# Six of the 52 maximum units of each head move from VectorE to ScalarE copies and 16-bit folds

## The reference, cut to what matters

```python
q = split(x @ Wq + bq); k = split(ctx @ Wk + bk); v = split(ctx @ Wv + bv)
attn = softmax(q @ k.T / sqrt(8))
out = attn @ v
```

## Time and profile before

| | |
|---|---|
| median of 3 runs | 4444.05 us (4439.82 to 4445.55) |
| the profiled execution's own time | 4451.81 us |
| its span, first to last instruction | 4449.9 us |
| TensorE busy | 3773.0 us, 85% of the span |
| VectorE busy | 3441.4 us, 77% |
| ScalarE busy | 2843.8 us, 64% |
| granted TensorE clock, mean | 0.891 of full speed |

### The profile page before, as it was taken

One profiled execution on the slowest core, in us unless ns is written; L12 is line 12 of the kernel. 1 busy time (PEld: TensorE's weight loads), 2 busy tenths in 40 slices (PEclk: granted clock), 3 DMA queues, 4 the chain that ended last, 5 costly groups with the idle time before them and its releaser, 6 DMA issues. The chain is left out here.

```text
span 4449.9 us, 83947 instructions
## 1 busy us (share of the span) xinstructions
PE 3773.0 (85%) x34296; PEld 1305.2 (29%) x34358; DVE 3441.4 (77%) x3306; ACT 2843.8 (64%) x4073; POOL 258.4 (6%) x183
## 2 busy tenths in 40 slices
PE   6898479999999964899999999289837999999996
PEld 2554122222222222222222222145412222222221
DVE  4332289999999814999999994489838999999981
ACT  0332238888888851688888888145423888888884
POOL 3000100000000000000000000234410000000000
PEclk9555669999999985899999999699966999999998
DMA  2000411111111013111111100200040111111100
GB/s 90 1 0 0 81 18 26 26 18 22 26 26 26 3 29 76 24 21 19 26 26 26 26 14 4 56 11 5 3 86 14 26 26 23 16 26 26 26 4 21
DMA packets 54250, 113.98 MB, mean 26 GB/s; under 512 B 9424, under 2 KB 44368, under 8 KB 48912
## 3 DMA queue, kind: packets, MB, share of 16 engines
q1 hardware_dynamic: 53904, 109.09, 13.7%
HBM read 83.46 MB, written 25.50 MB: 24 GB/s over the span
## 5 line engine op out<-in xcount | busy, mean ns | idle before, releaser
L1541 DVE TENSOR_REDUCE chunk_max<-max_scores 128x2 f32<-128x988 f32 (+1 forms) x2496 | 2790.8, 1178 | 188.1 <-PE max_scores L1424 152.3
L1522 ACT ACTIVATE probs<-scores 128x512 f32<-128x512 f32 (+1 forms) x3231 | 2452.7, 808 | 531.1 <-PE scores L1450 508.6
L1477 PE MATMUL values_sum<-probs,values 128*9 128x256 f32 x19584 | 1375.6, 383 | 26.7 <-DVE values_sum_s L1552 18.5
L1450 PE MATMUL scores<-queries,key_ring 49*128 49x512 bf16 x4800 | 1230.3, 385 | 51.2 <-ACT probs L1522 18.3
L1424 PE MATMUL max_scores<-key_ring,queries 48*128 48x494 bf16 (+1 forms) x4992 | 984.3, 392 | 157.5 <-DVE chunk_max L1541 112.9
L1477 PEld LDWEIGHTS values_sum<-probs,values 128*9 128x9 f32 x19584 | 376.6, 89 | 788.3 <-issue 566.7
L1450 PEld LDWEIGHTS scores<-queries,key_ring 49*128 49x128 bf16 x4800 | 308.0, 94 | 642.5 <-ACT probs L1522 543.0
L1424 PEld LDWEIGHTS max_scores<-key_ring,queries 48*128 48x128 bf16 x4992 | 241.0, 94 | 852.6 <-DVE chunk_max L1541 545.0
L1061 ACT ACTIVATE probs<-scores 128x512 f32<-128x512 f32 x256 | 138.4, 592 | 106.1 <-PE scores L1013 106.1
L1087 DVE TENSOR_REDUCE chunk_max<-max_scores 128x1024 f32 (+1 forms) x128 | 154.9, 1214 | 24.5 <-PE max_scores L969 24.3
L1552 DVE COPY values_sum_s<-values_sum 128x256 f32<-128x256 f32 x48 | 20.0, 416 | 183.8 <-PE values_sum L1477 183.8
(11 more groups left out here) (179 smaller groups left out, 2055.7 us busy)
## 6 DMA issues: line engine op xcount, KB each, us to landing
key_ring<-k_parts SPq DMA_DIRECT2D x96, 300.2 KB
key_ring<-k_parts SPq DMA_DIRECT2D x96, 200.1 KB
k_parts<-k_part SPq DMA_DIRECT2D x108, 128.0 KB, 2.3
key_ring<-k_parts SPq DMA_DIRECT2D x96, 100.1 KB
o_whole<-values_sum_s SPq DMA_DIRECT2D x48, 128.0 KB, 7.1
queries<-q_parts SPq DMA_DIRECT2D x36, 128.0 KB
context<-in_ctx_t SPq DMA_DIRECT2D x1, 3202.0 KB, 17.5
q_parts<-q_part SPq DMA_DIRECT2D x12, 256.0 KB, 2.8
```

Source lines behind the costliest of these rows:

```text
L1450: return pe.matmul(sc[:, g % 3, :], keys(rows, h, P * t, P * (t + 1)), qb[rows, q], start=True, stop=True)
L1477: mm = pe.matmul(acc[32 * b:32 * b + WV, 0:QBLOCK], vb[rows, h, t, :], pr[rows, slot, QBLOCK * (b % 2):QBLOCK * (b % 2 + 1)], start=(t == ...
L1522: act.activation(pr[:, a % RING:a % RING + b - a, :], sc[:, a % 3:a % 3 + b - a, :], ACT.Exp)\
L1541: dve.tensor_reduce(mx[:, h % 2, c, :, j], mxb[:, w % 2, :, 0:width], AX.X, ALU.max)\
```

## The change

Six units of every head are taken in another way: query tile pair 3 of chunks 1, 3, 5, 7, 9 and 11, every eighth unit. ScalarE copies such a unit from its `mxb` buffer to SBUF as bf16 (`copy_unit`). The first copy of a head goes to `max_of_copies`; VectorE folds each of the other five into it with one element-wise maximum of 16-bit operands (`fold_copy`). Behind the sixth, VectorE takes the maximum of the left and the right half (2 x 247 elements each) and then one TENSOR_REDUCE over 2 x 247. In VectorE's order the fold of a copied entry stands behind the reduce of the entry after it. In ScalarE's order the copy stands behind the Exp of operation `n + 1`, where `n` is the operation whose TensorE step holds the entry. TensorE waits for the copy, not for VectorE, before it refills that buffer. In the prologue the copies stand between the copies of the value projections. The buffer of chunk maxima is set to a low value once per cross attention, since for pair 3 not all of its cells are written any more.

```diff
+COPIED_TILE = 3
+COPIED_CHUNKS = (1, 3, 5, 7, 9, 11)
+LOWEST = -3.0e38
...
+def copied(w):
+
+    u = max_entry(w)[1]
+    return u is not None and u % 4 == COPIED_TILE and u // 4 in COPIED_CHUNKS
...
+def taken_through(w):
+    return w + 1 - COPIES_BEFORE[w + 1]
...
+        copy_of = sb("max_copy", [P, 2, 2, MAX_CHUNK], BF16)
+        copy_max = sb("max_of_copies", [P, 2, 2, MAX_CHUNK], BF16)
...
             def max_step(w):
                 h, u = max_entry(w)
-                if w >= 2:
-                    pe.wait_ge(max_taken, w - 1)
+                if w >= 2 and copied(w - 2):
+                    pe.wait_ge(unit_copied, COPIES_BEFORE[w - 1])
+                elif w >= 2:
+                    pe.wait_ge(max_taken, taken_through(w - 2))
...
+            def copy_unit(w):
+                h, u = max_entry(w)
+                c, x = u // 4, COPIES_BEFORE[w]
+                first = c == COPIED_CHUNKS[0]
+                act.wait_ge(max_scores, w + 1)
+                if first and h >= 2:
+                    act.wait_ge(head_max, h - 1)
+                elif not first and x >= 2:
+                    act.wait_ge(copy_folded, folds_through(x - 2))
+                dst = copy_max[:, h % 2] if first else copy_of[:, x % 2]
+                act.activation(dst[:, :, 0:max_width(c)], mxb[:, w % 2, :, 0:max_width(c)], ACT.Copy)\
+                   .then_inc(unit_copied, 1)
+
+            for c in range(3):
+                place_chunk(c)
+            for w in range(HEAD_UNITS + LEAD):
+                if copied(w):
+                    copy_unit(w)
+                if w % 4 == 3 and w // 4 + 3 < NCHUNK:
+                    place_chunk(w // 4 + 3)
             for n in range(NOPS):
...
                 act.activation(pr[:, a % RING:a % RING + b - a, :], sc[:, a % 3:a % 3 + b - a, :], ACT.Exp)\
                    .then_inc(exp_ready, 1)
+                if n >= 1:
+                    for w in range(entries_through(n - 2) if n >= 2 else HEAD_UNITS + LEAD, entries_through(n - 1)):
+                        if copied(w):
+                            copy_unit(w)
...
+            def fold_copy(w):
+                h, u = max_entry(w)
+                c, x = u // 4, COPIES_BEFORE[w]
+                whole, left, right = copy_max[:, h % 2], slice(0, MAX_CHUNK // 2), slice(MAX_CHUNK // 2, MAX_CHUNK)
+                dve.wait_ge(unit_copied, x + 1)
+                if c == COPIED_CHUNKS[0]:
+                    return
+                dve.tensor_tensor(whole[:, :, 0:max_width(c)], whole[:, :, 0:max_width(c)],
+                                  copy_of[:, x % 2, :, 0:max_width(c)], ALU.max).then_inc(copy_folded, 1)
+                if c == COPIED_CHUNKS[-1]:
+                    dve.wait_ge(copy_folded, folds_through(x))
+                    dve.tensor_tensor(whole[:, :, left], whole[:, :, left], whole[:, :, right], ALU.max).then_inc(halved, 1)
+                    dve.wait_ge(halved, h + 1)
+                    dve.tensor_reduce(mx[:, h % 2, c, :, COPIED_TILE], whole[:, :, left], AX.X, ALU.max)
...
             dve.memset(acc[:], 0.0).then_inc(acc_zeroed, 1)
+            dve.memset(mx[:], LOWEST).then_inc(lowest, 1)
...
                 while w < entries_through(last):
-                    take_entry(w)
+                    if copied(w):
+                        waiting.append(w)
+                    else:
+                        take_entry(w)
+                        for x in waiting:
+                            fold_copy(x)
+                        waiting.clear()
                     w += 1
```

More of the change, by code:

```diff
@@ L1316, in turn_entry, with folds_through, max_width @@
     return NENTRY - 1 if h == H - 1 else HEAD_UNITS + h * (HEAD_UNITS + 1) + TURN_AFTER
+def copied(w):
+    u = max_entry(w)[1]
+    return u is not None and u % 4 == COPIED_TILE and u // 4 in COPIED_CHUNKS
+COPIES_BEFORE = [0]
+for entry in range(NENTRY):
+    COPIES_BEFORE.append(COPIES_BEFORE[-1] + copied(entry))
+def taken_through(w):
+    return w + 1 - COPIES_BEFORE[w + 1]
+def folds_through(x):
+    per_head = len(COPIED_CHUNKS)
+    return (per_head - 1) * (x // per_head) + x % per_head
+def max_width(c):
+    return min(MAX_CHUNK, M - MAX_CHUNK * c)
 def tiles_through():
@@ L1356, in cross_attention @@
         head_max = sem("head_max")
+        unit_copied = sem("unit_copied")
+        copy_folded = sem("copy_folded")
+        halved = sem("halved")
+        lowest = sem("lowest")
         rows_loaded = sem("rows_loaded")
@@ L1380, in max_rows @@
             def max_rows(h):
-                sp.wait_ge(max_taken, turn_entry(h) + 1)
+                sp.wait_ge(max_taken, taken_through(turn_entry(h)))
                 for half in range(2):
@@ L1504, in place, with place_chunk @@
                                       src.rearrange("p (t h d) -> p t h d", t=count, h=H), ACT.Copy)
-            for c in range(NCHUNK - 1):
+            def place_chunk(c):
                 act.wait_ge(v_product, c + 1)
[L1508 to L1514, removed]
+                if c < NCHUNK - 1:
+                    place(slice(0, P), 4 * c, 4, sc[:, c % 3, :]).then_inc(v_copied, 1)
+                    return
+                place(slice(0, P), 4 * c, 2, sc[:, c % 3, 0:2 * P])
+                for half in range(2):
+                    rows = slice(32 * half, 32 * half + LAST_KEYS)
+                    place(rows, NTILE - 1, 1, sc[rows, c % 3, 2 * P:3 * P]).then_inc(v_copied, 1)
+            def copy_unit(w):
[17 more added lines that the diff above has]
+                    place_chunk(w // 4 + 3)
             for n in range(NOPS):
@@ L1539, in take_entry @@
                 c, j = u // 4, u % 4
-                width = min(MAX_CHUNK, M - MAX_CHUNK * c)
-                dve.tensor_reduce(mx[:, h % 2, c, :, j], mxb[:, w % 2, :, 0:width], AX.X, ALU.max)\
+                dve.tensor_reduce(mx[:, h % 2, c, :, j], mxb[:, w % 2, :, 0:max_width(c)], AX.X, ALU.max)\
                    .then_inc(max_taken, 1)
                 if u == HEAD_UNITS - 1:
-                    dve.wait_ge(max_taken, w + 1)
+                    dve.wait_ge(max_taken, taken_through(w))
                     dve.tensor_reduce(nmax[:], mx[:, h % 2].rearrange("p c g j -> p (g j) c"), AX.X, ALU.max,
                                       negate=True).then_inc(head_max, 1)
+            def fold_copy(w):
[4 more added lines that the diff above has]
+                if c == COPIED_CHUNKS[0]:
+                    return
+                dve.tensor_tensor(whole[:, :, 0:max_width(c)], whole[:, :, 0:max_width(c)],
[5 more added lines that the diff above has]
+                    dve.tensor_reduce(mx[:, h % 2, c, :, COPIED_TILE], whole[:, :, left], AX.X, ALU.max)
             def take_values(h):
@@ L1554, in _ @@
             dve.memset(acc[:], 0.0).then_inc(acc_zeroed, 1)
+            dve.memset(mx[:], LOWEST).then_inc(lowest, 1)
             dve.wait_ge(acc_zeroed, 1)
-            w = 0
+            dve.wait_ge(lowest, 1)
+            w, waiting = 0, []
             for h in range(H):
```

## The result

The changed kernel takes 4633.64 us (median of 4 runs, 4629.93 to 4639.45) against 4444.49 us: ratio 1.0425, 95% interval 1.0412 to 1.0438, so 4.25% slower, 189 us. The forecast was 4604 us, 160 us slower, with a range of 4460 to 4695. The profiled execution itself took 4636.54 us.

The account below looks back on a forecast made before the run. VectorE's maximum pass was taken to set the pace. Each cross attention adds 34.5 + 2.6 + 18 + 4.1, together 59 us; times 3 is 178, less 18 for filled idle time: +160, 4604 us, range 4460 to 4695.

Parts of the forecast that it names:

- The walk: Steady part: three copied units followed through the earlier trace, comparing later reduce starts before and after; weighted 0.46 us later.
- A: Copied unit with a one-slot Exp before its copy, copy in time: 0.49 us later; pattern of 30 of 90 units.
- B: Copied unit whose next unit is two steps on, TensorE already late: 0.13 us later; pattern of 20 of 90.
- C: Copied unit whose copy ends late behind a two-slot Exp: 0.61 us later; stands for 40 of 90 units.
- the filled gaps: VectorE's present idle times partly absorbing the delay: 0.08 us off for each of 225 units, 18 us in all.
- U-1: The unit before a copied one; behind its reduce VectorE waits for a refill, at the least 0.48 us.
- the late fold: In C the copy ends at 133.12, so the fold starts at 133.17 though VectorE is ready at 132.63.
- U+1: The unit after a copied one, sharing U-1's buffer; 0.5 to 0.9 us of idle time forecast before its reduce.
- U+2: The second unit after a copied one, refilling its buffer; its reduce start measures the lateness, weighted 0.46 us.
- rival 2: ScalarE's lateness after copies spreads through TensorE's scores: another 0.3 us in each of 288 units, +86, 4690; chance 0.13.
- Rival 3: VectorE's folds run at one element a cycle, as the f32 operation does: +125 us, 4729; chance 0.05.
- Rivals 1 and 4: Least waits, TensorE at hand, no late copy: 4465, chance 0.13; with half the idle time filled too: 4407, chance 0.08.

Follow-up runs that it names:

- small copies, no folds: The changed kernel with copies of 8 columns of each half instead of 494, without folds, halving and last reduce: 4433.7 us, ratio 0.9973.
- small copies, with folds: The changed kernel with copies of 8 columns, with folds, halving and last reduce at full width: 4537.52 us, ratio 1.0222.
- long copies, no folds: The changed kernel with its full copies, without the folds, the halving and the last reduce of each head: 4553.47 us, ratio 1.0258.
- folds in the gap: The changed kernel with each fold but a head's last moved in front of VectorE's idle time at the next copied unit: 4624.23 us, ratio 1.0411.

## Why the prediction was right, and which terms were not

**The sign, the size and the waits held.** The walk through units A, B and C forecast 55 us a cross attention in the steady part and 4 in the prologue, 160 in all with the filled gaps; it came to 189. The prices, the 0.48 us behind U-1, the late fold and TensorE held by the copy are in the trace as walked. The reading of the copies' table load (none comes) held too. The busy shares (87% against "about 88", 86% against "above 85") and the counts came as listed, and the idle time before U+1 is 0.72 us on the mean, from 0.47 to 1.23. "A head of about 63 us" did not: the 59.90 us of the earlier trace rows is one of the short heads. Heads 1 to 14 took 61.3 us on the mean and take 65.2, so 3.9 more, where 3.3 had been forecast.

**The walk held unit by unit.** From the start of the reduce of U-1 to that of U+2, the very units A, B and C took 3.29, 3.51 and 3.30 us before and take 3.76, 3.62 and 3.83: later by 0.47, 0.11 and 0.53, where the walk had 0.49, 0.13 and 0.61. Over the copied units of chunks 3, 5, 7 and 9 in heads 1 to 15 the patterns of A, B and C are later by 0.56, 0.28 and 0.56, 0.49 on the mean (forecast 0.46). First copies are later by 0.05 (0.17), and the sixth with the end of a head by 1.57 (0.46 + 1.2). So the nearness of the sum is not luck in the main.

**Two sizes were wrong.** The 18 us taken off for VectorE's idle times that get filled did not come: the steady parts grew by 173 us, against 165 forecast before that is taken off. And the pattern of C loses more behind U+2: 0.78 us by the start of U+4. That is the lateness that rival 2 named, smaller than its 0.3 us in each unit and in this pattern alone.

**What the walk is not good for.** The same walk can be done for the kernels of the experiments. Without folds every unit is like a first copy: 270 x 0.17 = 45, less the 18. With small copies (186 ns) C's refill of U+2 starts at 132.38 and its reduce at 132.80, 0.35 us early, and with a fold it starts at 132.63 + 0.59 = 133.22, 0.07 late. These estimates, added up as in the prediction:

| kernel | by the walk, us | measured, us |
|---|---|---|
| small copies, no folds | -69 | -12 |
| small copies, with folds | +90 | +99 |
| long copies, no folds | +27 | +115 |
| the changed kernel | +160 | +189 |

The walk is near where the folds load VectorE, and 57 to 88 us too low where they don't. It took the starts of TensorE and ScalarE as they had been and let VectorE's lateness alone count, "the maximum pass on VectorE sets the pace". So it prices the folds and ends of heads at 133 us and the copies' length without folds at 96; 74 and 127 were measured. A us of VectorE is worth 0.34 when taken away evenly, 0.37 to 0.56 when added, and 0.04 to 0.14 when taken away in one unit of eight (12 of 317, 40 of 289). The prediction named the coupling, gave ScalarE's part of it to rival 2 with 0.13, and put nothing of it in the sum. Rival 2's mechanism is shown, though not its size in the changed kernel: ScalarE's idle 17% didn't hide new work, neither on the kernel before (+59) nor with small copies and no folds (+89).

**Why folds in the gap gained nothing.** They cost almost nothing where they stood. Here is unit A without any folds, and then in the changed kernel:

```profile
2051.56 3.45 DVE L1598 TENSOR_REDUCE chunk_max<-max_scores 128x2 f32<-128x988 f32 x3 [0.90 <-PE max_scores L1459]
...
2052.11 0.38 PE L1459 MATMUL max_scores<-key_ring,queries 48*128 48x494 bf16 x2 [0.37 <-ACT max_copy L1559]
...
2055.34 1.19 DVE L1598 TENSOR_REDUCE chunk_max<-max_scores 128x2 f32<-128x988 f32 x1 [0.32 <-PE max_scores L1459]
```

```profile
2092.69 1.19 DVE L1600 TENSOR_REDUCE chunk_max<-max_scores 128x2 f32<-128x988 f32 x1 [0.90 <-PE max_scores L1459]
...
2093.79 0.66 DVE L1614 TENSOR_TENSOR max_of_copies<-max_of_copies,max_copy 128x988 bf16<-128x988 bf16 x1
...
2094.37 3.37 DVE L1600 TENSOR_REDUCE chunk_max<-max_scores 128x2 f32<-128x988 f32 x3
```

From the start of U+1 to the end of U+4 it takes 56.53 - 51.56 = 4.97 us without the fold and 97.74 - 92.69 = 5.05 with it (the 2000 left out). Without the fold VectorE waits for TensorE, whose refill of U+2 the copy had held, 0.32 us at U+4 alone. Over chunks 3 to 9 a fold adds 0.11, 0.09 and 0.02 us by the start of U+4 in the patterns of A, B and C, so moving four of them in each head can save some 13 us; the medians differ by 9. What the folds and the ends cost is the sixth unit's, 1.45 us late by U+4 against 0.39 without them (48 us in 45 heads), and the prologues' 12 us.

**Rival 3** (folds at one element a cycle) fell with 669 ns. Rivals 1 and 4 rested on TensorE being at hand, with 0.48 us before each U+1; it was 0.72 on the mean.

**Alignment.** The halving took 424 ns at an offset that is an odd multiple of two bytes. That is 0.42, the casts' pace, and not 0.67. Here the two pages of the Trainium skill differed: the trace agrees with its Vector Engine (DVE) Microarchitecture Reference, section 5.1 (alignment makes no difference), and not with the 4-byte condition in VectorE: DVE Perf Modes, Mode 2×_1P. The fold's 669 ns agree with the doubled rate that the latter's tier table gives a 16-bit tensor_tensor.

**What stays open.** Which part of the loop catches VectorE when it is relieved wasn't isolated: moving the maximum matmuls ahead of the values didn't free it. A ring of three buffers for the maximum scores, which might take the wait behind U-1 away, wasn't tried.

## What to carry to other kernels

An engine that is busy for 96% needn't be worth a us for each of its own: before moving work off it, narrow its instructions evenly and then all the way, and read what the time does (here -101 us for 293, and a floor 3.3 us a head below). In a ring of two buffers with one consumer, handing every eighth buffer to another engine makes the first wait for a refill it never waited for, and an engine's idle share doesn't hide new work that stands in a chain which others wait for. A walk through a few units of the trace priced the whole change well, but not its parts: work that is added behind a wait costs less than its length, and work that is taken away gives less.

## What the runs showed of the hardware that was not expected

Nothing out of the way: a 16-bit element-wise maximum of 988 elements ran in 669 ns and one of 494 in 424, with rows of 247 elements and a source at an odd 16-bit position; a TENSOR_REDUCE over 494 16-bit elements took 670 ns, what 494 f32 elements would take between the 176 ns measured for 16 and the 1181 for 988, so the narrow type alone sped nothing up there.
